# A shorter gather ring, output stores on another queue, and more sums added on GpSimd in a one-core transformer layer

## What is computed

```
x = layernorm(x + attn(x))                       # 16 x 256 tokens, 256 wide, 32 heads
topk_w, topk_ids = grouped_topk(x @ gate_w, bias)
buf[e, slot] = x[tok]                            # up to 48 rows for each of 64 experts
h   = silu(buf @ w_gate) * (buf @ w_up)
out = h @ w_down
y   = segment_sum(out[slots] * weights, tok)     # scatter-add back to tokens
x = layernorm(x + y + shared_expert(x))
```

## Time and profile before

| what | us |
|---|---|
| median of 3 runs | 1337.28 (1337.22 to 1339.1) |
| the profiled execution's own time | 1344.97 |
| its span, first to last instruction | 1343.1 |
| first part, up to the first gather | 1205.9 |
| first gather to first scatter | 26.5 |
| first scatter to the last one's landing | 69.3 |
| loads of the sums, second norm, stores | 41.4 |

### The profile page before, as it was taken

How to read it: one execution, slowest core, us unless ns; L and a number is a source line. 1 busy time by engine, 2 the same in 40 slices (tenths; PEclk the granted TensorE clock), 3 DMA queues, 4 the chain that set the end, 5 groups by cost and what they waited for, 6 DMA issues and landing times.

```text
span 1343.1 us, 39655 instructions
## 1 busy us (share of the span) xinstructions
PE 1296.6 (97%) x15292; PEld 1102.8 (82%) x15292; DVE 1031.0 (77%) x2344; ACT 922.9 (69%) x1738; POOL 482.0 (36%) x413
## 2 busy tenths in 40 slices
PE   7999999999999999999999999999999999997985
PEld 5788888888888888888888888888888888873564
DVE  6677879787878788787978787878878797874426
ACT  7667777777767777777777777777777777732425
POOL 0224243324233333424332423333342433335754
PEclk9999999999999999999999999999999999998998
DMA  8700000000000000000000000000000004486968
GB/s 305 261 2 10 28 9 21 15 1 27 9 27 10 27 9 27 10 27 9 24 13 1 27 9 27 18 27 17 27 18 27 17 19 126 133 265 160 237 109 314
DMA packets 48607, 82.17 MB, mean 61 GB/s; under 512 B 4849, under 2 KB 30545, under 8 KB 47569
## 3 DMA queue, kind: packets, MB, share of 16 engines
q1 hardware_dynamic: 39376, 66.64, 15.0%
q0 software_dynamic: 4608, 7.08, 3.0%
q10 hardware_dynamic: 4480, 6.29, 1.3%
HBM read 57.31 MB, written 22.69 MB: 60 GB/s over the span
## 4 chain that ended last, share of the span: by engine, by line
PE 85%; DMA 5%; DVE 4%; issue 2%; ACT 2%; SPq 1%; POOL 1%; DVEq 0%; ACTq 0%; POOLq 0%
PE pA L613 25%; PE pB L613 24%; PE pO L712 12%; PE pC L698 10%; PE pS L675 10%; DMA sums<-sb_stage,sb_sidx 3%; PE pC L613 1%; DMA sb_W<-sums 1%; DMA sb_stage<-wprep 1%; DVE sb_W L1253 1%; SPq L604 1%; ACT sb_W L969 1%; PE pB L897 1%; PE pC L737 1%; SPq L600 0%
## 5 line engine op out<-in xcount | busy, mean ns | idle before, releaser
L1758 POOL TENSOR_TENSOR sb_vl<-sb_v,sb_vh 128x512 f16<-128x512 f32 x121 | 154.2, 1274 | 680.2 <-ACT sb_vh L1015 680.2
L613 PE MATMUL pB<-sb_xh,sb_W 128*128 128x256 f16 x2048 | 350.4, 273 | 0.6 <-ACT sb_kh L997 0.5
L1304 DVE TENSOR_TENSOR sb_S<-pS,sb_D 128x1024 f32<-128x1024 f32 x248 | 235.9, 952 | 120.3 <-PE pS L675 120.3
L1023 ACT ACTIVATE sb_Shl<-sb_S 128x1024 f16<-128x1024 f32 x242 | 204.3, 844 | 110.7 <-DVE sb_S L1304 109.3
L613 PE MATMUL pB<-sb_xl,sb_W 128*128 128x256 f16 x1024 | 279.7, 273 | 0.0
L1310 DVE TENSOR_TENSOR sb_Shl<-sb_S,sb_Shl 128x1536 f16<-128x1536 f32 x121 | 225.3, 1862 | 10.5 <-ACT sb_Shl L1023 10.4
L613 PEld LDWEIGHTS pB<-sb_xh,sb_W 128*128 128x128 f16 x2048 | 200.3, 99 | 23.8 <-DVE sb_W L1253 0.8
L613 PE MATMUL pA<-sb_xh,sb_W 128*128 128x256 f16 x1024 | 175.8, 274 | 10.0 <-DVE sb_W L1253 5.6
L613 PE MATMUL pA<-sb_W,sb_xh 128*128 128x256 f16 x1024 | 175.9, 274 | 2.6 <-ACT sb_qh L990 2.6
L712 PE MATMUL pO<-sb_Wo,sb_yh 128*128 128x256 f16 x1016 | 173.3, 273 | 0.0
L1029 ACT ACTIVATE sb_gt<-pB 128x512 f32<-128x512 f32 x128 | 76.5, 598 | 140.4 <-PE pB L613 140.4
(11 more groups left out here) (361 smaller groups left out, 2700.9 us busy)
## 6 DMA issues: line engine op xcount, KB each, us to landing
sb_stage<-wprep SPq DMA_DIRECT2D x7, 1280.0 KB, 6.3
sb_W<-w_experts SPq DMA_DIRECT2D x17, 384.0 KB, 3.8
gather_rows<-sb_xr SPq DMA_DIRECT2D x16, 320.0 KB, 2.4
sb_W<-sums SPq DMA_DIRECT2D x10, 512.0 KB, 13.6
sb_xs<-xT SPq DMA_DIRECT2D x16, 256.0 KB, 2.9
sb_D<-decay SPq DMA_DIRECT2D x8, 512.0 KB, 7.5
sb_xn<-x SPq DMA_DIRECT2D x16, 256.0 KB, 3.1
sums<-sb_xr SPq DMA_DIRECT2D x16, 256.0 KB, 2.2
```

The costliest lines, as they stand in the source:

```text
L613: last = nc.tensor.matmul(dst, a, m, start=(i == 0), stop=(i == len(terms) - 1), **kw)
L1023: nc.scalar.activation(Sh[:, :, a:z_], S[:, :, a:z_], ACT.Copy).then_inc(s_Sh, 1)
L1304: nc.vector.tensor_tensor(scores_at(h)[:, :, a:z_], pS[:, :, a:z_], d[:, :, 0:z_ - a], ALU.mult).then_inc(s_Sm, 1)
L1758: nc.gpsimd.tensor_tensor(vl[q % 2][:, :, :], v32[:, :, :], vh[q % 2][:, :, :], ALU.subtract).then_inc(s_vl, 1)
```

## The change

The ring of gather buffers has eight places, all in `stage`, and five tiles are gathered before the loop in place of twelve. The four borrowed buffers are not used. SPLIT goes from 6 to 3. Chunks 2 and 6 move from VectorE's additions to GpSimd's. The 16 stores of the output are started by SP, after all of its loads of the sums, and no longer by ScalarE.

```diff
-XRING = 12
-AHEAD = 12
+XRING = 8
+AHEAD = 5
...
-BY_POOL = (1, 3, 5, 7)
-SPLIT = 6
+BY_POOL = (1, 2, 3, 5, 6, 7)
+SPLIT = 3
...
-        in_stage = carve(P, XRING - 4, ROW)
-        xg = [in_stage[:, r, :] for r in range(XRING - 4)] + [a[:, 0:ROW] for a in (y32, sq)]
-        xg += [a[:, :, :].rearrange("p t n -> p (t n)")[:, 0:ROW] for a in (xn, z)]
+        in_stage = carve(P, XRING, ROW)
+        xg = [in_stage[:, r, :] for r in range(XRING)]
...
+            for n, c in enumerate(ORDER):
+                sp.wait_ge(s_fo, n + 1)
+                sp.dma_start(out_t[c], fin[c][:, 1, :, :]).then_inc(s_out, 16)
             sp.wait_ge(s_out, 16 * FINALS)
...
                 last.then_inc(s_fo, 1)
-                act.wait_ge(s_fo, n + 1)
-                act.dma_start(out_t[c], fin[c][:, 1, :, :]).then_inc(s_out, 16)
```

## The result

The changed kernel took 1396.26 us (median of 3 runs, 1394.92 to 1399.39) against 1337.28 us: a ratio of 1.0436, interval 1.0419 to 1.0453. It is slower, by 59 us in the medians. The forecast was 1371 us with a range of 1352 to 1389, so the direction was right and the time lies outside the range, 25 us above the forecast.

The account below looks back on a forecast made before the run. The prediction took the chain of scatters, then the loads of the sums, to set the end. Its terms, +34.4 - 5.5 + 7.0 - 2.2 = +33.7 us on 1337.3, gave 1371.0 us, range 1352 to 1389.

Parts of the forecast that it names:

- The new ring of waits: Loop: each scatter hangs on the one two earlier through a whole gather and TensorE's transpose; adds 34.4 us.
- The size of a turn: Loop: one round of the scatter-to-scatter chain, giving two tiles, takes 9.4 us quiet and 10.2 us under weight loads.
- the third rival: Loop: gathers stay at 5.11 us and more, idle TensorE drops to 1.2 GHz; 19 us more, 1390; chance 0.08.
- The carried difference: Whole time: the median stays 7.7 us below the profiled execution, as in the kernel before.
- The gather under load: Loop: a gather takes 4.0 us from start to landing while weights are loaded, about six turns.
- Ahead of the loop: Before the first scatter: seven fewer gathers end TensorE's stall earlier; 5.5 us less, between 0 and 8.9.
- The late units: End: TensorE's late units, before run under the last scatters, lose that cover and delay chunk 8; 7.0 us more.
- The 14 chunks: End: the chunks left from chunk 8 on take 21.9 us in place of 24.05, 2.2 us less.
- Quicker gathers: Loop: all nine turns quiet, 8.9 us each, loop adds 25.1; 1362, or 1358 with the prologue's full 8.9; chance 0.12.
- GpSimd alone as the bound: Loop: TensorE never waits for a gather, GpSimd's own work sets the pace; 1333 us, faster; chance 0.06.
- Stores that do not pass: End: the stores do not pass behind the loads; up to 2 us, no chance of its own given.
- Slower still: Loop: six turns of 11.9 us plus one us on each of nine for TensorE's lower clock; 1390; chance 0.08.

Follow-up runs that it names:

- e3: Changed kernel with eight tiles gathered ahead in place of five, same ring of eight: 1347.87 us, ratio 1.0012.
- e4: Changed kernel with six tiles gathered ahead in place of five: 1358.32 us, ratio 1.0089.
- e12: Changed kernel with the ring of twelve buffers of before, still five tiles gathered ahead: 1395.35 us, ratio 1.0364.
- e6: Changed kernel plus 48 matmuls with unread results ahead of the transpose of each even tile from 6 to 22: 1386.23 us, ratio 1.0293.
- e7: Changed kernel without the eleven weight-pair loads beside the loop and TensorE's waits for them, output not the layer's: 1385.61 us, ratio 1.0298.
- e9: Changed kernel with eight tiles gathered ahead, chunks 1 to 4 ordered before chunk 8, GpSimd adding only 5, 6 and 7: 1344.20 us, ratio 0.9984.
- e11: Changed kernel with eight gathered ahead, chunks 1 to 4 before chunk 8, GpSimd adding 5 to 7, VectorE taking products of units 12 to 15: 1340.53 us.
- e2: Kernel before plus only the end part: stores from SP, SPLIT 3, six chunks added on GpSimd; twelve gathered ahead: 1344.47 us, ratio 0.9992.
- e14: Kernel before, twelve gathered ahead, with stores from SP, the other chunk order and products of units 12 to 15 on VectorE: 1344.45 us, ratio 0.9993.
- e1: Kernel before plus only the gather part: ring of eight, five tiles gathered ahead, old end: 1396.75 us, ratio 1.0369.

## Why the prediction missed

- **The new ring of waits: right.** Scatters in pairs, transposes of even tiles waiting for gathers, 41.7 us in all. e3, e4 and e12 show that the lead makes it: with A tiles ahead the chain closes over A - 3 tiles. At five it is two tiles in 12.4 us; at six three tiles, and 69.3 / 19 = 3.65 us a tile, 10.9 us for three (from an execution 4 us below the run's median); at seven, four tiles, 2.7 us a tile by that, and GpSimd's own 3.18 us for a gather and a scatter is the longer one: up to scatter 16, the last one with a gather ahead of it, a tile took 3.28 us, and the last three 2.66.
- **The size of a turn: the step that failed.** Its terms were 9.4 us quiet and 10.2 loaded; measured were 12.54 over five turns and 12.0 over all nine. It makes 18 us more than the 34.4 that the forecast had for the loop. Of the 2.3 us a turn too little, 1.86 are in the step from transpose to copy, taken at 3.02 us and measured at 4.88, and 0.53 in the gather and what follows it. The 3.02 us were the mean of 2.77 at a granted clock of 1.00 and 3.27, in which the trace of the kernel before shows a clock of 0.71: the slow clock was in that one, for part of the step, and the forecast averaged over it. The mechanism of the clock stood in the third rival, at one microsecond a turn and a chance of 0.08; e6 shows 1.6 a turn. The forecast itself had TensorE idle for half of each turn and kept the step near the speed of a busy one. In these traces the two don't go together, and the earlier trace rows had the price, 0.69 us against 0.38.
- **The carried difference: wrong too.** The forecast took its 7.7 us off the profiled time; the changed kernel's median and profiled time are equal. With the 17.4 us of the span this makes the 25 us. Without the 7.7 the forecast would have been 1378.7, the measured time 17.6 above it, and a range of the same width about it, 1360 to 1397, would just have taken the measured time in. So the turn made most of the error, and this difference took the time out of the range.
- **The gather under load: nearly right.** 4.0 us taken, 4.40 measured. e7 shows that the crossing weights make it: 3.18 without them, the 3.2 us worked out from the earlier trace rows. The load ended after six turns, as I had taken it: tile 16's gather still took 4.97 us, those of tiles 18, 20 and 22 took 3.15, 3.28 and 3.01. That turns stayed above 11 us up to scatter 17 all the same is again the step from transpose to copy, 3.84 to 5.35 us in the last three, at a granted clock of 0.50 to 0.56.
- **Ahead of the loop: right within its bounds.** -7.1 for -5.5. With six to nine gathers (the changed kernel, e3, e4, e9 to e11) the first scatter stands 18.5 to 21.1 us behind the first gather, with thirteen 26.1 to 26.7 (before, e2, e14). That it is the gathers' traffic which holds TensorE there agrees with this but was not isolated. One thing priced at nothing appeared as a wait and was hidden by 7.00 us of idling: GpSimd's sixth gather waited for the shared expert's stores, `sums<-sb_gt`:

```profile
1217.34 0.94 POOL L1812 DMA_INDIRECT sb_stage<-gather_rows,sb_gidx  x1 [4.90 <-DMA sums<-sb_gt]
1225.29 1.64 POOL L1819 DMA_INDIRECT sums<-sb_stage,sb_sidx  x1 [7.00 <-DVE sb_stage L1688]
```

- **The late units: right, too small by 1.8 us.** The last copy came 7.25 us behind scatter 19 (6.2 taken) and chunk 8 another 23.5 us later (23.0 taken). e3 shows the same loss with a loop as short as before; e9 and e11 show that it is paid only by what stands behind chunk 8 in VectorE's order.
- **The 14 chunks: right in size, wrong in origin.** 21.24 us for 21.9. But e1, which has the old end, needs 20.28 us for them: what makes these chunks quick is that the loads come early against the late units, and the moved additions and the stores behind the loads gave nothing that shows.
- **Rivals.** Quicker gathers: no, none in the loop of the changed kernel was under 2.9 us. (That rival's turn is 8.8 us by its own terms, not 8.9, which makes it 1361.) GpSimd alone as the bound: not at five ahead, but nearly at seven. Stores that do not pass: they passed, and nothing hung on it. Slower still: its clock was real, at up to twice its price, its gathers of 5.11 us were not (4.97 at most).

## What to carry to other kernels

When a change lets a busy engine wait, its own steps have to be priced as that engine runs after idling: here TensorE's step rose from 2.8 us at full clock to 4.9 us, and the transfers in the turn, no longer hidden, took 4.4 us where other traffic crossed them and 3.2 where none did. What a short lead cost per tile here was the round trip divided by the tiles it covers (6.2 us at five ahead, 3.65 at six); from seven on, where that fell below GpSimd's own work per tile, more lead brought little: 60.5, 58.6 and 58.2 us for the loop at seven, eight and twelve. If some work loses its cover, look at what stands behind it in the in-order engines: losing the cover took the end stretch from 38.7 us (e2) to 47.7 (e3), and putting other chunks ahead of the late ones brought it to 37.2 (e11).

## What the runs showed of the hardware

- Idle times of 4.5 us in front of a transpose left TensorE at a granted clock of 0.50 for all of the even tile's step (3.9 us at 1256.90 in the changed kernel). The length of the last idle time alone did not decide it: two transposes took 0.41 us, full speed, behind 3.14 us of idling (e7, tile 10) and 0.66 us behind 2.87 us (changed kernel, tile 18). Matmuls without a use raised the clock of the five turns from 0.73 to 0.97 and made the kernel 9 to 10.5 us faster (e6).
- An indirect gather of 164 KB behind a scatter landed after 2.95 to 3.5 us in e7 with no other loads; in the changed kernel the even tiles' gathers took 3.7 to 5.0 us while weights were loaded, though the DMA engines had a mean share of only 0.55 in the five turns. The Trainium skill (DMA: Bandwidth & Descriptors, Anatomy of one DMA, SWDGE path) would give an estimate of 2.4 us for this size; even in e7 no gather was that short, the shortest being 2.95 us.
